# New turn orders for the five engines of a macaron block (expert layer, windowed attention, expert layer)

## The reference

```
x = x + 0.5 * ffn(layernorm(x))
x = x + attn(layernorm(x))
x = x + 0.5 * ffn(layernorm(x))

ffn:  scores = softmax(x @ Wg + bg);  the best 2 of 8 experts per token
      h = gelu(x @ W1[e] + b1[e])  (512 wide);  y = h @ W2[e] + b2[e];  out = sum of prob * y
attn: 16 heads of 8; each token sees itself and the 8 tokens before it in its sequence
      softmax(q.k / 0.56) over these 9, times v, then @ Wo
```

## Time and profile before

| | |
|---|---|
| median of 3 runs | 1034.41 us |
| the profiled execution's own time | 1039.25 us |
| its span, first to last instruction | 1037.5 us |
| busy PE / DVE / ACT / POOL | 842.0 / 643.9 / 500.8 / 671.5 us |
| granted clock of TensorE, mean | 0.933 |
| scatters of rows (L595) | 256, 306.6 us |
| scatters of results (L609) | 305, 356.3 us |

### The profile page before, as it was taken

How to read it: one execution, slowest core, us unless ns; L and a number is a source line. 1 busy time by engine, 2 the same in 40 slices (tenths; PEclk the granted TensorE clock), 3 DMA queues, 4 the chain that set the end, 5 groups by cost and what they waited for, 6 DMA issues and landing times.

```text
span 1037.5 us, 22518 instructions
## 1 busy us (share of the span) xinstructions
PE 842.0 (81%) x6345; PEld 736.0 (71%) x6345; DVE 643.9 (62%) x1309; ACT 500.8 (48%) x1215; POOL 671.5 (65%) x593
## 2 busy tenths in 40 slices
PE   4348996899789999988999649888987959966973
PEld 3247895898578877876778536777876948955973
DVE  4876354334489988989899989688871602300232
ACT  4546753474355547557365145644335625433431
POOL 3586777668788884456786466357867667665552
PEclk9999988999989999999999879999996989997996
DMA  9414333832155211461121211422222235732873
GB/s 293 131 46 114 84 76 86 199 78 70 52 108 142 58 48 29 102 138 35 35 57 40 96 58 38 77 63 70 55 61 67 66 79 126 163 113 58 211 167 130
DMA packets 170488, 96.44 MB, mean 93 GB/s; under 512 B 137712, under 2 KB 154406, under 8 KB 169604
## 3 DMA queue, kind: packets, MB, share of 16 engines
q1 hardware_dynamic: 152420, 59.29, 24.7%
q0 software_dynamic: 17952, 35.71, 11.6%
HBM read 25.77 MB, written 52.35 MB: 75 GB/s over the span
## 4 chain that ended last, share of the span: by engine, by line
PE 26%; DVE 15%; issue 9%; DMA 7%; SPq 7%; POOL 5%; ACT 2%; ACTq 0%; DVEq 0%; POOLq 0%
PE bank L983 10%; PE bank L966 7%; POOL x_sorted L595 5%; DMA x_sorted<-hl,slots_all 3%; SPq L473 3%; PE bank L881 2%; DVE prod L1175 2%; DVE prod L1221 2%; PE bank L854 2%; PE bank L868 2%; DVE prod L1186 2%; DMA xsT<-x_sorted 2%; DVE y_sb L1440 1%; SPq L477 1%; DMA y_in<-y_pairs 1%
## 5 line engine op out<-in xcount | busy, mean ns | idle before, releaser
L609 POOL DMA_INDIRECT y_pairs<-y_sb,tile_ids x305 | 356.3, 1168 | 198.1 <-issue 150.4
L595 POOL DMA_INDIRECT x_sorted<-hl,slots_all x256 | 306.6, 1198 | 153.3 <-issue 79.5
L770 ACT ACTIVATE h_f<-bank,b_cols 128x256 f32<-128x256 f32 (+1 forms) x736 | 264.3, 438 | 283.9 <-PE bank L966 278.2
L983 PE MATMUL bank<-w_sb,h_f 128*128 x2440 | 322.5, 284 | 2.4 <-ACT h_f L770 2.3
L983 PEld LDWEIGHTS bank<-w_sb,h_f 128*128 128x128 f32 x2440 | 297.9, 197 | 8.6 <-issue 4.3
L966 PE MATMUL bank<-xsT,w_hl 128*128 128x256 f16 (+1 forms) x2208 | 253.6, 265 | 58.1 <-DMA xsT<-x_sorted 56.5
L966 PEld LDWEIGHTS bank<-xsT,w_hl 128*128 x2208 | 196.8, 102 | 92.4 <-issue 66.3
L1440 DVE TENSOR_TENSOR y_sb<-bank,tile_ids 128x256 f32<-128x256 f32 (+1 forms) x184 | 68.3, 374 | 200.0 <-PE bank L983 197.5
L1221 DVE TENSOR_TENSOR prod<-score,qkv 128x2304 f32<-128x2304 f32 x32 | 81.6, 2549 | 0.2
L1175 DVE TENSOR_TENSOR prod<-qkv 128x2304 f32<-128x2304 f32 x32 | 81.4, 2551 | 0.2
L881 PE MATMUL bank<-prod,ident 128*128 128x256 f32 x288 | 69.6, 393 | 3.3 <-DVE prod L1221 2.9
(11 more groups left out here) (159 smaller groups left out, 847.9 us busy)
## 6 DMA issues: line engine op xcount, KB each, us to landing
y_in<-y_pairs SPq DMA_DIRECT2D x28, 512.0 KB, 5.2
x_sorted<-no_rows SPq DMA_DIRECT2D x7, 720.0 KB, 4.8
y_pairs<-y_sb,tile_ids POOLq DMA_INDIRECT x305
x_sorted<-hl,slots_all POOLq DMA_INDIRECT x256
x_sorted<-no_rows SPq DMA_DIRECT2D x56, 72.0 KB, 1.6
x_sb<-in_L_attn_x SPq DMA_DIRECT2D x3, 1024.0 KB, 6.5
out<-x_sb SPq DMA_DIRECT2D x3, 1024.0 KB
xsT<-x_sorted SPq DMA_TRANSPOSE x184
```

The lines of the kernel that those rows point to most:

```text
L595: pool.indirect_dma_start(out=x_sorted[p], out_offset=bass.IndirectOffsetOnAxis(ap=slots_all[:, at:at + 1], axis=0), in_=hl[:, c % 2, i // ...
L609: pool.indirect_dma_start(out=y_pairs, out_offset=bass.IndirectOffsetOnAxis(ap=tile_ids[:, t.n % IDS, i, 0:1].bitcast(U32), axis=0), in_=y ...
L770: ins = act.activation(h_part(t, b)[:, k, :], bank[h_banks.uses[u][0]][:, k * t.slots:(k + 1) * t.slots], ACT.Gelu, bias=b1_cols[:, bass.d ...
L983: ins = pe.matmul(into[:, half, :], h_part(t, c // t.per)[:, c % t.per, half * P:(half + 1) * P], w2_flat[:, bass.ds((e * HC + c) * D, D)] ...
```

## The change

Only the five strings change. Every stream has the same turns in the same sequence, and every engine issues the same number of instructions; each string only mixes the streams in a new way. Steps, waits, buffers and PSUM banks stay.

```
 PE_ORDER = (
...
-    "aapaappaaapppaappaapppppppppaaaepapraaaeeaeeeeepeeereeeeeeereeeeeeerererererereeeeeeereeaaaeeaeeeeeeeeeeeeeeea"
-    "eeeeeeeeaeeeaeaaaeeeeeeaaeaaeaaaeeeaaeaaeaaaeeeeeaaeaaeeeeeeeeerererrerereererereeeeeereeeeeeeeeeeeeeeeeeeeeee"
...
+    "aaaaaaappppppaapppappapppepaaappaapaeepaaereeeepereeeereeereereeerereereereeeeeeeeereaaeeeaeeeeeeeeeeeaeeeeeee"
+    "eaaeaeeeeeaeeeeaaeeeaeaeeeaeaaaaeeeaaaeeeaeaaaeeaeaeaeaeeeeeeeeeeeeeeereeeeeeeerereereerereereeerereeeeeeeeree"
...
 DVE_ORDER = (
...
-    "aeaaeaeaaeaeaeaaeaeaearererereaaaarahhappaaaaappapphphaaaaaarahaaahraarrraarrrraraaahahaaeaaeaaeaeaaeaaearerre"
...
+    "aeaaeaaaeaaeaaeaeaearerreaaaerrehaeahaeaaaaaappaaaappappphhaaaaarrrrhrahraraarrraaaaaaaaeaaehaeaaeaahaeaerrrer"
...
 ACT_ORDER = (
...
-    "eaappphppppaapppaapppprrrhrrhrrrreeeraeeerereereereeereereeaeeaaraahppaapppppphppppppaapppppppppppeprrrhrrhrrr"
...
+    "peepppapapepppaapppreprrephrrhrrrrpreareererrereeepeereeaaeaeereeaaaahhppppppppppppppappppapppppprprrrhrerprep"
...
 POOL_ORDER = (
-    "sssssyysyysyyyyyyyyyyyyyysyyyyyysyyyyyyyyyysyyyyyyyyysysysyyyyysyyyyyyyyyysyyysyyyyyyyyyyyyyssssssssyyyyyyyyyy"
-    "yyyyyyyyyyssssssssyyyyyyyysyysyyyysyyyssssyyyyyysyyyyyysyyyyyyyyyyysssyyyyyyyyyyyysyyyyyysssyyyyyyyyyyyyyyyyyy"
+    "ssssssyyyyyyyysyyyyyyyysyyyyyyyyssyyyyyyyysyyyyysyyysyyyyysyyyyyyyyyyyyyyyyyssyyyyyyyyyyyyyysyssysyysysssyyyyy"
+    "yyyyyyyysyysssssssyyyyyyyssyyyyysysyyssyyyysyyyyysyyyyyyyysyyyyyysyysysyyysyyyyysyyyyyyyssyyyyyyyyyyyyyyyyyyyy"
     "yyyyyyyyyyyy"
 )
 SP_ORDER = (
-    "tttttttttttttttttttttttttttttyyttttyytttttttttttttttttttttttyytttyyttttttttttttttttttyyttttyytttttttttttttttyy"
-    "yytttttttttttttttttttttttttttttttttttttttttttttttttttttyytttyytttyttttttttttttyytttyytttyyytttyytttytttttyyyyy"
+    "ttttttttttttttttttttttttttttytyttyytttttttttttttttttttttyytttyyttttttttttttttttttttttytyyyttttttttttttttttttyy"
+    "yytttttttttttttttttttttttttttttttttttttttttttttytyttttytttyyyyttytttttyttttttyttttttytttttyytttttttttyttyyyyyy"
     "yyy"
 )
```

More of the change, by code:

```diff
@@ L87 @@
-    "peeppeeeeeeeeeeeeeeepepeepepeepepeepepeeeeeeeeeeepppp"
+    "rrrrrrhhrrrrrrhhrrrrrrrrhrrhrrrrrhhrrrhrrhrrhhrreerrrrererrehreeheeeeereheeeherrreehreerreheerhrrrrrerpehpepep"
+    "pepeperhheeeeeherrehreheeeereaahhrehaaaaahahaaeaeaeaaaeaaepapeaeppeppepeaaeaaaeaaaeaaaaeraaeaeaaaaaheraaheaaaa"
+    "aaeararareaaaahahaaaeaaeaaeaeaeaeaerraraeapeaperrehapepapeppeaahaeaaaaeaaahaaaaahhaaaeaaaaaahaarrraaaaaehhaaaa"
+    "aeaaeaaaeaaeaaeaeaearerreaaaerrehaeahaeaaaaaappaaaappappphhaaaaarrrrhrahraraarrraaaaaaaaeaaehaeaaeaahaeaerrrer"
```

38 lines of the change are left out of this document (17 added, 21 removed).

## The result

In 20 runs of each on one chip the kernel before took 1037.82 us and the changed one 1042.86 us: ratio 1.0053, 95% interval 1.0031 to 1.0075; one of the 20 executions of the changed kernel took 4516 us and is not in the ratio. The change makes the kernel slower by half a per cent; forecast was a gain of 20 us. The profiled execution has a span of 1038.8 us against 1037.5 and a mean granted clock of 0.926 against 0.933. Single executions are a coarse measure here: kernels with the same strings up to 769 us differ there by up to 3.6 us (-0.2 to +3.4). So I read a shift against the shift at the entry of its stretch, and leave the verdict to the ratios. The one trace of before is itself such an execution.

A forecast was written before the change was run, and what follows sets the result against it. The bound changes by stage: DVE in attentions, POOL's string pacing tiles. Stage shifts chain to -20 us, all by tile 160, with the tail zero; from 1034.4 that gives 1014.4, stated as 1015, range 1000 to 1032.

The forecast's parts named there:

- First attention: Pass 3's low-half wait moved, -3 us, and fewer e turns, about -3: attention 0 ends 6 us early.
- eleven e turns fewer ahead of the first projection: In the first attention, fewer e turns before the first projection, less the few returning by its end: about -3 us.
- Pass 4's rows: Five wide results between the bursts, +5 us, and later gates, +3: low half of pass 5, chunk 1, shifts +1.
- Gates of pass 5: Gates right behind the slots on DVE, -6.0 us, fewer result turns, -1.6: first scatter at 576.5 instead of 583.82.
- Last attention's start: ACT's high half of pass 5, chunk 3, comes ahead of group 3's normalising: keys at 632, shift 0.
- End of attention 3: Tile 96 no longer holds up channel sums on PE, softmax some 6 us earlier: attention 3 ends at 769.1 - 5.
- Routes of pass 7: Behind the last attention, rank 7 shifts -3 to -5 us; tile 127's result comes at 823, -13.5.
- Pass 7's rows: From tile 127's result to the last row scatter 95.5 us instead of 102.5; tile 160's load at 921.4, -20.
- Tail: Store of group 2 no longer stretches a tile's load, -3 us, but precedes the last loads, +3 to +4: zero.
- POOL's string paces the tiles: SP's tile loads wait for the result scatter eight tiles earlier: 118.8 us in all, once 59.0.
- the gains of the middle do not arrive: Rival, chance 0.28: pass 5's rows start where they did, only the order around pass 7 pays; 1020 to 1032 us.
- stretched scatters: Rival, chance 0.15: pass 4's ten moved scatters all run under DVE products, +14.4 us; middle 1045 us.

The follow-up runs named there:

- the fourth stretch: Kernel before with old strings up to the results of tile 116 and the new ones behind, to the end: ratio 0.9897.
- third stretch: Kernel before with new strings only from the start of the last attention up to the results of tile 116: ratio 1.0043.
- first stretch: Kernel before with new strings up to the end of the first attention and start of the second, old ones behind: ratio 1.0061.
- s_front: Kernel before with new order up to DVE's first products of keys, all other turns in the old sequence: ratio 0.9993.
- s_back: Kernel before with old order up to DVE's first products of keys, then the new sequence to about tile 67, then the old string: ratio 1.0158.
- g_gate5: Kernel before with slots, gates and first gate column of pass 5 earlier on DVE and its first burst behind tile 93 on POOL: ratio 1.0002.
- second stretch: Kernel before with new strings only from the end of the first attention to the start of the last: ratio 1.0001.
- q_late: New strings from pass 7 on, but second-layer combinations, loads and stores of groups 0 and 1 at their old places: ratio 0.9961 to before.

## Why the prediction was wrong

The forecast's shifts are taken apart by stage here, from the two columns of the table above; the last column is the same stage in the run that has it alone. For the result of tile 127 that is the fourth stretch; the third, which reaches to tile 116, adds +2.3 there. The traces add up to +1.3 us, the 20 runs to +5: the trace of before is 1.4 us over the median of its kernel, that of the changed one 2.3 under it.

| stage, up to | forecast | all new | error | alone |
|---|---|---|---|---|
| end of attention 0 | -6 | +8.8 | **+14.8** | +6.6 |
| low half 5.1 | +7 | +7.4 | +0.4 | +10.0 |
| gates of pass 5 | -8 | -7.4 | +0.6 | -7.4 |
| keys of attention 3 | +7 | +4.9 | -2.1 | +5.2 |
| end of attention 3 | -5 | -5.4 | -0.4 | +0.1 |
| result of tile 127 | -8.5 | -3.9 | +4.6 | -8.5 |
| load of tile 160 | -6.5 | +2.0 | **+8.5** | +3.8 |
| end | 0 | -5.1 | -5.1 | -6.1 |
| sum | -20 | +1.3 | +21.3 | |

**First attention: the step failed, in sign.** I priced the moved wait for a low half at -3 and "eleven e turns fewer ahead of the first projection" at -3 more. The attention ended 8.8 us late in the whole and 6.6 late with the first stretch alone, where twelve kernels with the old strings up to there lie between -1.0 and +4.3; the ratio of that stretch, 1.0061, says the same. The wait moved, as written; but it was not what bound, for with it taken out the attention ended no earlier (+8.2). What I did not follow were the loads and combinations of group 1, four tiles earlier on SP and DVE, which now meet results that have not landed. s_front and s_back show that the loss is in this part of the strings; that these loads are its cause is read from DVE's and SP's waits and was not shown, since the trial made for it stalled elsewhere. The rival for this side was missing; I had half a sentence on the first layer.

**Pass 4's rows: size right, by luck in part.** Results cost 17 us against 12.7 forecast, because two of ten scatters met a product: 4 us more, close to the third of 14.4 that the prediction called its mean case and left out of the sum. The filled waits give 9.2 against 8. So the bursts came as late as I had it, but they were not what made the low half late: with them and the gates put back it still loses 7.9 us from the end of attention 0 on. The low half came at +16.2 and not at +1 because of what was carried in.

**Gates of pass 5: right.** From the low half to the gates the whole gains 7.4 us where I had 8; the step on DVE moved alone gives 3.8. (The forecast's own sum there, 583.82 - 6.0 - 1.6 + 1, is 577.2 and not 576.5.)

**Last attention's start: size right, reason half wrong.** I let the gates' gain be eaten by ACT's early high half (5.1 us). It does stand there, 12.05 us in the whole. But where "POOL no longer idles its 6.40 us" I did not ask what stands behind the burst: in g_gate5 POOL waits 8.34 us for the gates with two results behind it, and where ACT was untouched these two places on POOL decided between 1.0002 and 0.9951. I took a loss for given that can be avoided.

**End of attention 3: size right, reason not borne out.** I had -5 because channel sums no longer stand behind tile 96 on PE; the whole has -5.4. But the stretch that holds this new order alone has +0.1, and kernels with the old order there gain as much when only the keys come late: from +9.2 to +3.7 in the second stretch alone, from +4.9 to -2.2 in g_gate5. That the number fits is luck.

**Routes of pass 7: right where nothing is carried in** (-8.5; -10.8 with the high half behind the exponentials; ten kernels with the old strings there lie between -2.7 and +0.1). In the whole the last scatters of pass 6 come 16.3 us late, 8.7 of them in the third stretch alone against 2.6 at the end of its attention, and ACT's high half 7.1, now ahead of the last two tiles of tokens, waits for them. Rank 7, which I used as a sign (-3 to -5), came at +26.2; with 12 us of it taken away, 2.3 us were gained at tile 127 and nothing in the ratio.

**Pass 7's rows: the step failed at one number, "tile 159 at 918.96 - 13.5 = 905.5".** I recounted POOL's queue for the last row scatter, and carried the shift over unchanged for the results up to tile 151, which SP's loads of tile 159 follow. Six bursts stand between the results of tiles 127 and 151 now, where four stood. From tile 127 to tile 151 the shift grows by 7.8 us in the whole (+4.4 to +12.2) and by 7.1 where POOL's string alone is new (-0.6 to +6.5). From there to the load of tile 159 it grows by 3.7 more, where I had 3. The chain to the last row scatter shrank by 2.9 us (102.5 to 99.7) where I had 7: POOL's waits in it, 16.6 us before, are still 7.8, not 4. That SP's clearing is late next was right: 8.02 us of it stand between tiles 159 and 160. From the end of attention 3 to tile 160 the early loads and combinations cost some 4 us against q_late, in one trace each.

**Tail: 0 was wrong by some 2 us.** The table has -5.1, but kernels with the old tail have -1.8 to -4.8 there, 3.2 in the mean, so about 2 us belong to the change (about 3 in the fourth stretch alone). I priced the store against the last loads at +3 to +4. The trial of the store alone shows no such price; q_late, which loses 4.7 us there where the others gain, shows that the work done early in part 5 is what the tail saves.

The premise that "POOL's string paces the tiles" was read from one row of SP's waits. Two more rows of that view in before are nearly as large:

```profile
SPq L473 <- PE bank L966: 120.8, 36, 13.4
SPq L467 <- DMA x_sorted<-hl,slots_all: 93.0, 7, 21.3
```

SP waits as long for PE to give a tile's buffer free as for results eight tiles back. With POOL's string alone new from tile 116 on the ratio is 0.9989, with all strings 0.9897, so POOL's order by itself is not what sets the time there.

So two steps failed, the order inside the first attention, forecast at -6 and measured at +6.6 alone, and the results up to tile 151, forecast to move with tile 127 and found 7 to 10 us later in the whole and in the kernels with POOL's new string; the second is followed to its bursts, the cause within the first stays open.

Of the rivals, "the gains of the middle do not arrive" gave 1020 to 1032, below the 1042.86 measured, and named one reason of several. The slower one, stretched scatters, had 1044 to 1045 and +15 to +20 at the keys of group 3, which is nearly what came (+13.7); that is luck, for only two of its ten scatters were stretched.

## What to carry over

When a step is moved ahead on one engine, list what now stands behind it on every in-order queue that the same step touches: the gates' early place was worth 0.5% or nothing, decided by two results behind a burst on POOL. A wait that a trace shows is a price only if its removal moves the next hand-over; two of the most visible ones here (8.2 us of DVE, 12 us of rank 7) moved nothing that could be measured at the end. Read each stage also in kernels that did not change it: here they showed 3 us of a supposed gain to be the trace of before. Cut a change of orders into stretches at points where both versions have issued the same turns, keep the stretches that gain, and move single steps back only in a schedule that is not late already.

## What the runs showed of the hardware

Executions of one kernel spread by 13 us (1032.75 to 1045.52 in 20 runs of before), and identical strings part early: between 260 and 290 us the granted clock lay between 0.84 and 0.99 and PE finished 100 to 112 matmuls, in kernels that do not differ there. A scatter's length on POOL goes by what DVE runs when it begins: 0.95 to 1.00 us where DVE runs nothing (248 in before), and until 0.83 to 0.88 us after the end of a running product of keys or values (59 of 59 in before, 51 of 51 in the changed kernel). Of the ten results moved into attention 1 two met one, so the surcharge was 4 us where ten would be 14.
